# The last two blocks' tail: one tile split for ScalarE and GpSimd, one for GpSimd alone, and two early steps moved by a tile

## The reference, cut to what matters

```python
P = x @ U1                     # rank 32
H = gelu(P @ V1 + b1)          # 512 hidden features
Q = H @ U2                     # rank 32
out = x + Q @ V2 + b2
```

## Time and profile before

| | us |
|---|---|
| median of 3 runs | 871.35 (871.04 to 872.43) |
| the profiled execution | 872.09, of which the span of instructions is 870.3 |
| TensorE busy in the span | 863.0 |
| VectorE busy | 675.2 |
| ScalarE busy | 568.4 |
| GpSimd busy | 403.9 |

### The profile page before, as it was taken

The page is one execution under the profiler, slowest core; times in us unless marked ns, Lnnn a source line. Parts: engine busy times, 40 slices in busy tenths (PEclk is TensorE's granted clock), DMA queues, the critical chain, the costliest instruction groups (busy, mean ns, idle before and its releaser), DMA issues.

```text
span 870.3 us, 12522 instructions
## 1 busy us (share of the span) xinstructions
PE 863.0 (99%) x3814; PEld 690.2 (79%) x3814; DVE 675.2 (78%) x1109; ACT 568.4 (65%) x1024; POOL 403.9 (46%) x373
## 2 busy tenths in 40 slices
PE   9999999999999999999999999999999999999997
PEld 5778888777888888888888888888888887777774
DVE  7877777979689687686686686686665789998987
ACT  7788888765555455555555555555555668989896
POOL 7457783134356453252252353343224427664563
PEclk9999999999999999999999999999999999999999
DMA  9689980024113112012012012011010049582600
GB/s 314 219 260 309 310 267 33 4 84 137 50 49 125 44 43 85 1 49 85 1 49 85 1 50 84 1 49 49 0 49 1 1 74 197 143 196 50 171 14 36
DMA packets 36115, 82.01 MB, mean 94 GB/s; under 512 B 4432, under 2 KB 14416, under 8 KB 34256
## 3 DMA queue, kind: packets, MB, share of 16 engines
q1 hardware_dynamic: 35616, 80.96, 30.4%
q10 hardware_dynamic: 432, 0.26, 0.1%
HBM read 70.32 MB, written 6.83 MB: 89 GB/s over the span
## 4 chain that ended last, share of the span: by engine, by line
PE 89%; DVE 5%; issue 2%; ACT 2%; SPq 2%; DMA 1%; POOL 0%; DVEq 0%; ACTq 0%; POOLq 0%
PE ps L954 19%; PE ps L959 18%; PE ps L973 18%; PE ps L1016 9%; PE ps L1014 9%; PE ps L1009 9%; PE ps L996 3%; PE ps L994 2%; DVE HL L1702 1%; SPq L791 1%; PE ps L989 1%; ACT HH L1023 1%; DVE Hf L1687 1%; PE ps L929 1%; DMA ST<-in_wa_dram 0%
## 5 line engine op out<-in xcount | busy, mean ns | idle before, releaser
L1131 ACT ACTIVATE Sg<-ps 128x512 f32<-128x512 f32 x288 | 172.1, 597 | 243.5 <-PE ps L973 242.9
L1677 DVE TENSOR_TENSOR Hf<-ps,Sg 128x512 f32<-128x512 f32 x288 | 198.1, 688 | 141.6 <-ACT Sg L1131 88.1
L1806 POOL TENSOR_TENSOR HL<-Hf,HH 128x512 fp32r<-128x512 f32 x133 | 179.1, 1355 | 171.1 <-ACT HH L1023 161.3
L1023 ACT ACTIVATE HH<-Hf 128x512 fp32r<-128x512 f32 x343 | 214.5, 625 | 16.0 <-DVE Hf L1677 8.7
L1702 DVE TENSOR_TENSOR HL<-Hf,HH 128x512 fp32r<-128x512 f32 x241 | 211.1, 876 | 2.6 <-ACT HH L1023 1.6
L954 PE MATMUL ps<-XHL,WBH 128*128 128x512 f32 x512 | 203.3, 397 | 0.1
L959 PE MATMUL ps<-XHL,WBL 128*128 128x512 f32 x512 | 202.5, 396 | 0.0
L973 PE MATMUL ps<-XHL,WBH 128*128 128x512 f32 x512 | 201.6, 394 | 0.0
L1821 POOL TENSOR_TENSOR XT<-XT,TMP 128x512 f32<-128x512 f32 x64 | 83.4, 1303 | 223.9 <-DVE TMP L1524 223.7
L954 PEld LDWEIGHTS ps<-XHL,WBH 128*128 128x128 f32 x512 | 96.2, 188 | 24.4 <-DVE Hf L1677 1.2
L973 PEld LDWEIGHTS ps<-XHL,WBH 128*128 128x128 f32 x512 | 96.6, 189 | 22.5
(11 more groups left out here) (293 smaller groups left out, 1316.9 us busy)
## 6 DMA issues: line engine op xcount, KB each, us to landing
CWB<-scratch SPq DMA_DIRECT2D x14, 1024.0 KB, 4.7
GWD<-expert_down SPq DMA_DIRECT2D x20, 576.5 KB, 4.8
GWU<-expert_up SPq DMA_DIRECT2D x20, 514.0 KB, 5.2
CWB<-scratch SPq DMA_DIRECT2D x40, 256.0 KB, 5.5
ST<-in_wb_dram SPq DMA_DIRECT2D x8, 768.0 KB, 6.2
ST<-scratch SPq DMA_DIRECT2D x24, 256.0 KB, 8.0
GX<-XT SPq DMA_DIRECT2D x66, 64.0 KB, 3.0
XT<-in_x_dram SPq DMA_DIRECT2D x8, 256.0 KB, 5.7
```

Of the source, the lines that this page charges most:

```text
L1023: e.activation(HH[:, it.n % NH, 0:it.cols], hidden_place(it), ACT.Copy).then_inc(s_hi_act, 1)
L1131: e.activation(Sg[:, it.n % NG, :], zb[z % NZ][:, :], ACT.Silu).then_inc(s_act, 1)
L1677: e.tensor_tensor(Hf[:, it.n % NS, :], zb[z % NZ][:, :], Sg[:, it.n % NG, :], ALU.mult).then_inc(s_prod, 1)
L1806: e.tensor_tensor(HL[:, it.n % NH, :], Hf[:, it.n % NS, :], HH[:, it.n % NH, :].bitcast(F32), ALU.subtract).then_inc(s_lo_pool, 1)
```

## The change

It has four parts.

1. F7.1 is no longer whole. It gets the same treatment as F7.3: HH by ScalarE, HL by GpSimd, two fp32r matmuls.
2. F6.3 is no longer whole. GpSimd makes both halves, HH with a new copy and then HL; two fp32r matmuls.
3. Softmax step 6 for g = 1 stands one slot later on VectorE.
4. The four gates matmuls stand behind the up-projection of their slot.

```diff
-        self.whole = kind == "F" and (f % 2 == 1 and (blk, f) != (NBLK - 1, 3) if blk >= LATE else (blk, f) in ((0, 1), (2, 1)))
+        self.whole = kind == "F" and (f % 2 == 1 and (blk, f) not in ((NBLK - 2, 3), (NBLK - 1, 1), (NBLK - 1, 3)) if blk >= LATE else (blk, f) in ((0, 1), (2, 1)))
...
-            for step, slot in ((0, 0), (2, 1), (3, 1), (4, 2), (5, 3), (6, 3 + g)):
+            for step, slot in ((0, 0), (2, 1), (3, 1), (4, 2), (5, 3), (6, 3 + 2 * g)):
...
+            it.hi_pool = False
             if it.whole:
...
-            end = (it.kind, it.blk, it.f) == ("F", NBLK - 1, 3)
+            end = it.kind == "F" and it.blk == NBLK - 1 and it.f % 2 == 1
+            it.hi_pool = (it.kind, it.blk, it.f) == ("F", NBLK - 2, 3)
+            if it.hi_pool:
+                it.hi_act, it.lo_pool = False, True
+                n_lo_pool += 1
+                hi[it.n], lo[it.n] = (s_hi_pool, 1), (s_lo_pool, n_lo_pool)
+                continue
...
             for k in range(slots):
-                if k == g_gates:
-                    ...
                 ...
                 if k < len(items) and items[k]:
                     up(e, items[k])
+                if k == g_gates:
+                    ...
...
                 if 1 <= k <= len(items) and items[k - 1] and items[k - 1].lo_pool:
                     it = items[k - 1]
+                    if it.hi_pool:
+                        e.wait_ge(*hidden(it))
+                        e.wait_ge(s_down, it.n - NH + 1)
+                        e.tensor_copy(HH[:, it.n % NH, :], Hf[:, it.n % NS, :]).then_inc(s_hi_pool, 1)
```

More of the change, by code:

```diff
@@ L238, in build @@
         s_gated = sem("s_gated")
-        s_hi_act, s_hi_dve = sem("s_hi_act"), sem("s_hi_dve")
+        s_hi_act, s_hi_dve, s_hi_pool = sem("s_hi_act"), sem("s_hi_dve"), sem("s_hi_pool")
         s_lo_dve, s_lo_pool = sem("s_lo_dve"), sem("s_lo_pool")
@@ L892, in tensor_program @@
                     up(e, items[k])
+                if k == g_gates:
+                    bk = ab_bank("t")
+                    e.wait_ge(*small.of("table"))
+                    e.wait_ge(s_index, 1)
+                    e.wait_ge(s_pairs, 2)
+                    for x in range(4):
+                        mm = e.matmul(bk[:, 264 + NPAIR:264 + 2 * NPAIR], S("ones")[0:NB, :], pairs[0:NB, 1, x, :],
+                                      start=x == 0, stop=x == 3)
+                    mm.then_inc(s_small, 1)
                 if k == g_in:
@@ L1694, in vector_program @@
                     h, f, l = HH[:, it.n % NH, c], hidden_place(it), HL[:, it.n % NH, c]
-                    if not it.hi_act and it.border != 7:
+                    if not it.hi_act and not it.hi_pool and it.border != 7:
                         e.wait_ge(*hidden(it))
```

## The result

The changed kernel takes 873.60 us in the median (873.18 to 875.26, 16 runs) against 871.91 of the kernel before (871.04 to 873.37, 16 runs): a ratio of 1.0022, 95% interval 1.0015 to 1.0030. In time that is 1.3 to 2.6 us more; the medians are 1.69 apart. The profiled execution took 873.18, its span is 871.4.

The account below looks back on a forecast made before the run. TensorE, busy 99% and without a gap in its last 9 us, was taken as the bound. End queue +1.86, gates 0 and softmax step 0 on the median 871.35 gave 873.2; range 870.9 to 874.0.

Parts of the forecast that it names:

- rival 4: The end's queue plus the new gates wait passed on by the groups behind, +0.3 to +0.5 on top: 873.6; chance 0.07.
- rival 1: At the end, VectorE and GpSimd stand in one queue for SBUF: +1.86 us, 873.2 (872.6 to 873.9); chance 0.70.
- the close call: At the end, GpSimd's HL F6.3 (860.36) was taken ahead of VectorE's HH F7.0 (860.39); the other order gives +1.70.
- the three offsets: A waiting VectorE copy ends 0.28, a VectorE HL 0.55 behind GpSimd's end; a waiting GpSimd HL 1.15 behind VectorE's.
- both QS that "aren't held": VectorE's QS, reading PSUM and one SBUF tile, isn't held by GpSimd: 0.73 at 859.73, 0.75 at 865.61.
- TensorE's -0.80: Splitting F6.3 and F7.1 takes 0.40 each from TensorE's matmuls, 0.80 at most, if the halves are there.
- rival 2: Added GpSimd work at the end doesn't hold up VectorE; only GpSimd's own chain counts: -0.45, 870.9; chance 0.15.
- TensorE's waits: At the end, TensorE waits about 1.2 for HL F7.0, about 1.3 for HL F7.2, and for HH F7.2 between.
- Rival 3: At the end only one split costs, the other's HL finding a gap; F7.1 alone +0.73, 872.1; chance 0.08.
- The chain behind: After the last low matmul the chain is as before; QS of block 7 isn't held up, cover 0.3 us.
- The gates: Near 40 us, a wait of about 0.26 for GpSimd's GHL replaces 0.18; value 0, bounds -0.2 and +0.2.
- The softmax step: On VectorE near 197 us, moved past the next product; wait at 196.5 stays; value 0, bounds -0.1 and +0.1.

Follow-up runs that it names:

- e5: Changed kernel with F7.0 and F7.2 left in PSUM, where VectorE reads them for HH and HL: 871.21 us, ratio 0.9996 to the kernel before.
- e7: Kernel before, F6.3 and F7.1 whole, but GpSimd also makes both halves of F6.3, which nobody reads: 872.48 us, ratio 1.0005.
- e2: Kernel before with only F7.1 made as two halves (HH by ScalarE, HL by GpSimd), F6.3 left whole: 872.67 us, ratio 1.0013.
- e1: Kernel before with only F7.1 and F6.3 made as two halves, gates and softmax step as before: 873.36 us, ratio 1.0022.
- e8: Changed kernel with F6.2, F7.0, F7.2 and F7.3 in PSUM, VectorE making HL F7.3 instead of GpSimd: 871.26 us, ratio 0.9992 to the kernel before.
- e4: Kernel before with only the softmax step a slot later and the gates matmuls behind the up-projection: 871.56 us, ratio 1.0000.
- e6: Changed kernel with F7.0, F7.2 and F7.3 in PSUM, VectorE making HL F7.3 instead of GpSimd: 870.92 us, ratio 0.9990 to the kernel before.

## Why the prediction was right

It said 873.2 with 870.9 to 874.0; measured were 873.60. It was built on a median of 871.35, and over more runs that of before is 871.91; the predicted +1.86 stands against a measured +1.69 of the medians and +1.84 of the tail. That 873.60 is to the hundredth the figure of rival 4 is chance: its mechanism fell (see below), and 0.56 of the figure is the higher median of before. The forecast gave "slower by over 0.2%" 0.46 and "within 0.2%" 0.50; the measured interval (1.0015 to 1.0030) lies on both sides of that bound. And it had no term for TensorE's clock, although the five runs at 0.996 may hold some 0.2 of the 1.69 (without them the medians are 1.51 apart). By its steps:

- **The queue (rival 1).** Right, instruction by instruction. From the mark, the prediction had the last low matmul at 866.41 - 857.71 = 8.70, measured 8.67. GpSimd was first at the close call (859.62 against VectorE's 859.66), as taken; the three offsets (0.28, 0.55, 1.15) held in each meeting to about a hundredth: HL F7.3 ended at 864.03, 1.14 after HL F7.0's end at 862.89. e5 shows that it is the meeting on SBUF and not the amount of work, e7 that it works with TensorE's gain taken away. One reading behind it proves less than it says: both QS that "aren't held" ran while GpSimd was idle (859.25 to 862.60, and after 863.87). The changed kernel has the case: QS at 859.00 took 0.73 beside GpSimd's copy (858.48 to 859.55), so the statement was right.
- **TensorE's -0.80.** The work did go, but it doesn't reach the end, as it would have in rival 2 (870.9). For F6.3, e7 shows that none of it does (7.59 against 7.58): the waits that stand in its place swallow it. For F7.1 that was not tried by itself; by the rows TensorE, through with F7.1, waits 0.63 for HH F7.2 (864.36 - 863.50 - 0.23), more than the 0.40 saved.
- **TensorE's waits.** Predicted were about 1.2 for HL F7.0, which is right, and 1.3 for HL F7.2, which isn't. The idle times in the rows (1.02, 0.46, 0.22) count from the modelled end of the matmul before, 0.39 after its start, while the next one can start after 0.23. By the starts HL F7.0 came 862.94 - 861.53 - 0.23 = 1.18 late, HH F7.2 0.63, and HL F7.2 0.39 (865.09 - 864.36 - 0.34). I had put the whole second lateness on the low matmul, though HH F7.2 takes the greater part of it. HL F6.3, said to come in time, was also a little late (0.50 at 860.97 in TensorE's timeline). The sum doesn't rest on these sizes, and they close it: 0.80 saved, 1.18 + 0.63 + 0.39 = 2.20 waited, and 0.11 at each of the four matmuls that were waited for, make +1.84.
- **Rival 3, only one of the parts costs.** It fell: each costs (0.73 and 0.74). The 7.57 of its working for F7.1 alone was met in e2 to the hundredth.
- **The chain behind.** QS of block 7 was not held up: it starts at 866.73, when PH is ready, with VectorE idle for 0.37 (0.3 had been the cover). From the last low matmul to the end of the span it is 5.7 before and after, so "moves the end by the same amount" held here. It isn't a rule: in e1 and e8 it didn't.
- **The gates.** As worked out, a wait of 0.27 (0.26 had been said) in place of 0.18, and no more; **rival 4**, that it would be passed on, fell with e4 (1.0000, tail 6.83). **The softmax step** was worth nothing either; the wait at 196.5 is still there (now at 195.72), since the product behind the long HL is as late as before. Of the changed kernel's timelines, VectorE's HL and TensorE's L961 (they answer to the earlier trace rows):

```profile
193.49 1.57 DVE L1709 TENSOR_TENSOR HL<-Hf,HH 128x512 fp32r<-128x512 f32 x1
...
195.72 0.50 PE L961 MATMUL ps<-XHL,WBH 128*128 128x512 f32 x1
```

- **What it did not speak of.** The profiled executions reach the mark up to 1.7 us apart (856.77 to 858.43) in kernels whose first 850 us are nearly the same. One place is seen. The waits of e1 from 52 to 56 us (engine, what was waited for: us, times, longest):

```profile
ACT GHL L1116 <- DMA GX<-XT: 1.6, 1, 1.6
PEld ps L961 <- DVE HL L1709: 1.5, 1, 1.5
```

The tokens of a group came late by DMA. This wait is 1.6 in e1, 1.3 in e7 and 0.6 in the profiled execution of before, and these reach the mark at 858.43, 858.25 and 857.71. Of the seven without it, five (the changed kernel's among them) are there at 856.77 to 857.12. The other two, e6 and e8, are there only at 857.76 and 857.95, so it isn't the only cause. The first up-projection of the changed kernel's execution was also 0.47 earlier than that of before (4.73 against 5.20), but it is at 4.74 in e1 too. The two together would cover the lead of 0.73; I haven't followed the way between. The DMA wait isn't the change's doing, since e1 and e7 have the early part of before and waited longest; what sets it from run to run stays open.

## What to carry to other kernels

Idle time of GpSimd is not free when VectorE's work in the same stretch reads SBUF twice or copies from it: price the added instruction by the queue of both engines, in the order of issue, and only then subtract what another engine saves. At 128x512, a VectorE copy that waited ended 0.28 and a VectorE subtraction 0.55 us behind GpSimd's end; a GpSimd copy ended 0.47 and a GpSimd subtraction 1.15 behind VectorE's. If the work must go there, leave VectorE's operand in PSUM: here that turned a tail 1.84 us longer than before into one about 0.4 shorter (6.47 against 6.84), though the copy itself is dearer (0.68 against 0.41). And compare short tails from a mark inside the trace, since whole executions of one kernel differ by more than such an effect (871.04 to 873.37 for the kernel before); but then see that the part behind the tail has kept its length.

## What was not expected of the hardware

The granted clock of TensorE fell in the tail of e1 from the 2.4 to the 1.2 GHz level after about 4 us with 2.53 busy, which made its last matmuls 0.63 instead of 0.40 long, the tail 0.45 longer and what follows it another 0.5. The changed kernel, with the same waits up to the same matmul and 2.52 busy in the same four microseconds, kept 1.00 until 868 us.
